# Layer-norm normalising on ScalarE, scale and shift on GpSimd, loads issued one by one, and a new timetable in a two-layer attention and expert kernel

## The chip, the cores and the metric

The kernel runs on one core of a Trainium2 chip. The metric is the device time of one execution in microseconds (us); lower is better. The core has TensorE (PE, its weight loads PEld), VectorE (DVE), ScalarE (ACT), GpSimd (POOL) and SyncE (SP), which here only issues DMAs.

## What is computed

Two pre-norm transformer layers run over x of shape (8, 512, 128), eight batches of 512 tokens of width 128. The reference, cut to its frame:

```python
def _layernorm(x, axis=-1, eps=1e-05):
    m = jnp.mean(x, axis=axis, keepdims=True)
    v = jnp.var(x, axis=axis, keepdims=True)
    return (x - m) / jnp.sqrt(v + eps)

x = x + _L0_attn_ref(_layernorm(x), wq, wk, wv, wo)          # causal, 16 heads of 8, 4 key heads
x = x + _L0_ffn_ref(_layernorm(x), router_w, router_b, w1, w2)     # 8 experts, top 1, silu(a) * g
x = x + _L1_attn_ref(_layernorm(x), W_q, W_dkv, W_uk, W_uv, W_o, ln_gamma, ln_beta)  # latent of 32, own norm, rotary
x = x + _L1_ffn_ref(_layernorm(x), gate_w, gate_b, w1, b1, w2, b2) # 8 experts, top 2, relu
```

The latent of layer 1's attention (512 x 32 a batch) is normalised too, and then multiplied by ln_gamma and shifted by ln_beta.

## The kernel before

The residual X stays in SBUF, 128 tokens of a tile on the partitions, 4 tiles a batch. Attention goes batch by batch, 16 in all (8 of layer 0, then 8 of layer 1). Each batch has a preparation (`prep`: statistics, normalise, transpose, projections, splitting q and k into three bf16 parts, parking these in DRAM and loading them back as stacks), a first pass over the scores for the row maxima (`max`, `m_hi`, `m_mid`, `m_park`, `m_load`), a second pass with Exp and the values (`score`, `values`, `normalise`), and the output projection (`turn_ctx`, `project`). After `project` comes the second norm of the layer (`stats`, `norm`, `turn` with x = "half") and the router's logits. The experts work on half the tokens at a time: group g = 0 is batches 0 to 3, g = 1 batches 4 to 7. When the fourth batch of a group is through, DVE chooses experts and places (`route`, `choose`, `places`), POOL scatters the rows in expert order to DRAM (`scatter`, 16 indirect DMAs in layer 0, 32 in layer 1), SP loads them back four tiles at a time (`fetch`), PE works slot by slot (`first`, `second`; 23 slots a group in layer 0 and 39 in layer 1, with a weight fetch `fetch_w1` each), and POOL gathers the results (`combine`, 16 or 32 indirect DMAs), each added to X by DVE. Layer 1's attention of a group needs layer 0's `combine` of that group. The kernel ends with layer 1's `combine` of g = 1 and its stores.

There are 40 layer norms: 16 of x = "xn" and 16 of "half" (four tiles of 128x128 each) and 8 of "lat" (four of 128x32). Each is: DVE bn_stats and bn_aggr on four tiles and var + eps (L1488 to L1493); POOL pow(-0.5) over 4 columns (L1025 to L1027); POOL four times (x - mean) * rs (L1049 to L1050), for "lat" also times gamma (L1054) and plus beta (L1056); PE transposes the result (L1125 or L1167). The small statistics have two buffers (`ln_small`), `xn` has one.

Every engine runs a list of steps of its own, in order, fixed when the kernel is built. `schedule()` gives each step a nominal time from constants (FIRST_SCORES, LENGTHS, AHEAD, HURRY, SCATTER, EXPERTS_AFTER, SLOT, COMBINE, W1_AHEAD). `Plan.make_orders` then simulates the engines with the costs in PARTS and the landing times in LANDS, and puts next the step that could start first; a tie goes to the lower nominal time. So nominal times are priorities, and costs decide which steps look ready. Only `set_ones`, `load_rest`, `fill` and `load_expert` (NOT_BEFORE) aren't put ahead of their nominal time. On the chip a step waits on semaphores, and what stands behind it on its engine waits too.

`load_rest` is a single step of SP at nominal 40.0: it issues 21 DMAs in a row, X of batches 2 to 7 and 15 weight and table loads (L886 to L893). The `fill` steps (L895 to L900) write zeros to the DRAM that the scatters go to, 10 DMAs of up to 512 KB, of which FILLS puts four at nominal 10 to 13.

## Time and profile before

| what | value |
|---|---|
| median of 3 runs | 1159.88 us (1159.86 to 1162.81) |
| the profiled execution's own time | 1159.01 us |
| its span in the trace | 1157.0 us |
| PE busy | 960.1 us, 83% |
| DVE busy | 696.5 us, 60% |
| POOL busy | 575.4 us, 50% |
| ACT busy | 562.1 us, 49% |

Busy time says how much an engine did, not what the end waited for. For that there are three views: the busy time of each engine in chosen stretches (where PE isn't full, something else holds the work up), the chain that ended last (followed back from the last instruction, at each step to what released it), and the instructions of one engine in order of time. Shares of the chain are given for a stretch. An SPq line is SP's time issuing DMAs.

### The profile page before, as it was taken

How to read it: one execution, taken by the hardware profiler on the slowest of the kernel's cores; microseconds unless marked ns; L12 is line 12 of the kernel's file. 1: busy time of each engine (PE TensorE's matmuls, PEld its weight loads, DVE VectorE, ACT ScalarE, POOL GpSimd, SP SyncE). 2: the span in 40 equal slices, each digit the busy share in tenths (PEclk: the TensorE clock that was granted, in tenths of full speed). 3: DMA queues.
4: the chain of work that ended last, by engine and by line, in shares of the span. 5: the costliest groups of instructions: out<-in, count | busy, mean ns of one | idle time of the engine just before them, and what ended most of it. 6: DMA issues, size and time to landing. Idle time of an engine off the chain costs nothing.

```text
span 1157.0 us, 26493 instructions
## 1 busy us (share of the span) xinstructions
PE 960.1 (83%) x9732; PEld 632.6 (55%) x9732; DVE 696.5 (60%) x1414; ACT 562.1 (49%) x987; POOL 575.4 (50%) x752
## 2 busy tenths in 40 slices
PE   3578889987999988887999988897989998887930
PEld 2334444544878545343887644443444687877930
DVE  2867776886556885778645787779768233123112
ACT  1056557663444443471454545454657854544610
POOL 4055544456211699456222399646884425455046
PEclk9999998987999988796999978897889999989975
DMA  4805432326654114316655204223441257778722
GB/s 135 191 26 160 111 94 68 90 63 185 205 161 124 49 50 112 84 58 176 197 159 160 52 20 121 85 59 79 139 121 53 69 145 205 217 219 239 199 67 73
DMA packets 148045, 139.42 MB, mean 121 GB/s; under 512 B 35056, under 2 KB 126544, under 8 KB 147920
## 3 DMA queue, kind: packets, MB, share of 16 engines
q1 hardware_dynamic: 141776, 125.13, 39.8%
q0 software_dynamic: 6144, 12.60, 3.8%
q8 instruction: 82, 1.34, 0.5%
q14 instruction: 43, 0.35, 0.1%
HBM read 94.82 MB, written 42.86 MB: 119 GB/s over the span
## 4 chain that ended last, share of the span: by engine, by line
PE 46%; POOL 21%; issue 10%; DVE 8%; DMA 6%; SPq 5%; ACT 5%; POOLq 0%; ACTq 0%; DVEq 0%
PE psum L1299 11%; PE psum L1232 9%; PE psum L1309 7%; POOL sorted_in L1095 7%; PE psum L1214 4%; POOL gathered L1105 4%; DVE neg_max L1452 4%; PE psum L1190 3%; ACT scratch L1398 3%; POOL scratch L1082 3%; POOL xn L1050 3%; DMA gathered<-sorted_out,rows_of 3%; PE psum L1161 2%; PE psum L1242 2%; POOL xn_half L1050 2%
## 5 line engine op out<-in xcount | busy, mean ns | idle before, releaser
L1452 DVE TENSOR_REDUCE neg_max<-psum 128x2 f32<-128x768 f32 (+3 forms) x352 | 382.6, 1120 | 103.5 <-PE psum L1195 101.1
L1398 ACT ACTIVATE scratch<-psum 128x1024 f32<-128x1024 f32 x320 | 317.5, 1027 | 122.7 <-PE psum L1214 121.3
L1082 POOL TENSOR_SCALAR_AFFINE_SELECT scratch<-scratch 128x512 f32<-128x512 f32 x256 | 159.4, 642 | 275.3 <-ACT scratch L1398 274.9
L1190 PE MATMUL psum<-k_stack,q_stack 48*128 48x128 bf16 (+3 forms) x1024 | 162.2, 339 | 47.9 <-DVE neg_max L1452 21.2
L1232 PE MATMUL psum<-scratch,values 128*32 128x512 f32 (+3 forms) x2048 | 183.3, 484 | 12.0 <-POOL scratch L1082 7.2
L1299 PE MATMUL psum<-rows_t,w_now 128*128 128x128 f32 x1360 | 176.1, 281 | 4.4 <-issue 1.9
L1299 PEld LDWEIGHTS psum<-rows_t,w_now 128*128 128x128 f32 x1360 | 163.4, 195 | 15.5 <-issue 13.0
L1309 PE MATMUL psum<-w,hidden_t 128*128 x992 | 139.7, 285 | 16.4 <-DVE rows_out L1449 12.3
L1214 PE MATMUL psum<-q_stack,k_stack 51*128 51x512 bf16 (+3 forms) x1024 | 126.2, 319 | 27.8 <-ACT scratch L1398 12.1
L1105 POOL DMA_INDIRECT gathered<-sorted_out,rows_of x96 | 92.8, 967 | 97.3 <-DMA sorted_out<-rows_out 66.1
L1309 PEld LDWEIGHTS psum<-w,hidden_t 128*128 128x128 f32 x992 | 123.5, 196 | 27.8 <-issue 27.2
L1434 ACT ACTIVATE hidden_t<-psum,w_now 128x128 f32<-128x128 f32 x312 | 88.4, 370 | 84.1 <-PE psum L1299 66.2
L1190 PEld LDWEIGHTS psum<-k_stack,q_stack 48*128 48x128 bf16 x1024 | 54.3, 101 | 117.9 <-issue 40.1
L1193 PE MATMUL psum<-masks_bf 64*128 64x128 bf16 x1024 | 118.3, 242 | 0.0
L1095 POOL DMA_INDIRECT sorted_in<-xn_half,rows_of x96 | 93.5, 974 | 46.8 <-issue 26.0
L1232 PEld LDWEIGHTS psum<-scratch,values 128*32 128x32 f32 x2048 | 59.2, 117 | 86.6 <-issue 53.0
L1195 PE MATMUL psum<-masks_bf 64*128 64x64 bf16 x1024 | 104.4, 206 | 0.0
L1449 DVE TENSOR_TENSOR rows_out<-psum,w_now 128x128 f32<-128x128 f32 x78 | 22.6, 292 | 115.0 <-PE psum L1309 114.9
L1317 ACT ACTIVATE ctx_raw<-psum 128x512 f32<-128x512 f32 x64 | 38.2, 597 | 103.2 <-PE psum L1232 103.1
L1214 PEld LDWEIGHTS psum<-q_stack,k_stack 51*128 51x128 bf16 x1024 | 36.7, 97 | 92.4 <-issue 39.9
L1195 PEld LDWEIGHTS psum<-masks_bf 64*128 64x128 bf16 x1024 | 58.5, 109 | 35.2 <-issue 14.0
L1679 DVE SCALAR_TENSOR_TENSOR X<-gathered,gate,X 128x128 f32<-128x128 f32 x96 | 38.2, 398 | 62.6 <-DMA gathered<-sorted_out,rows_of 60.9
(115 smaller groups left out, 1108.3 us busy)
## 6 DMA issues: line engine op xcount, KB each, us to landing
w_now<-in_w SPq DMA_DIRECT2D x78, 322.0 KB, 3.6
w_now<-in_w SPq DMA_DIRECT2D x46, 512.0 KB, 4.1
q_stack<-q_parts SPq DMA_DIRECT2D x64, 192.0 KB, 4.3
sorted_out<-rows_out SPq DMA_DIRECT2D x60, 128.0 KB, 3.5
rows_in<-sorted_in SPq DMA_DIRECT2D x28, 256.0 KB, 3.4
q_parts<-q_parts SPq DMA_DIRECT2D x16, 384.0 KB
k_stack<-k_parts SPq DMA_DIRECT2D x32, 192.0 KB, 3.7
sorted_in<-gathered SPq DMA_DIRECT2D x8, 512.0 KB, 5.1
```

Of the source, the lines that this page charges most:

```text
L1082: pool.affine_select(out=diag, in_=diag, compare_op=ALU.is_ge, fill=0.0, base=0, pattern=[[0, 4], [1, P]], channel_multiplier=-1).then_inc ...
L1095: pool.indirect_dma_start(sorted_in[g][:, :], bass.IndirectOffsetOnAxis(ap=rows_of[g][k][:, t:t + 1], axis=0), xn_half[:, t, :], None).the ...
L1105: pool.indirect_dma_start(gathered[s.slot][:, :], None, sorted_out[g][0:SLOTS[s.layer] * P, :], bass.IndirectOffsetOnAxis(ap=rows_of[g][k] ...
L1190: pe.matmul(out[:, j * width:end], q_stack[i][rows, pair, t * P:(t + 1) * P], k_stack[i][rows, k_of(layer, pair), 0:width], start=True, st ...
L1193: pe.matmul(out[:, end - P:end], ident_up[half, :], mask_up[half, :], start=False, stop=False)
L1195: ins = pe.matmul(out[:, end - P // 2:end], ident_low[half, :], mask_low[half, :], start=False, stop=True)
L1214: ins = pe.matmul(bank[u.bank + k][:, off:off + SEQ - j * P], k_stack[i][rows, k_of(layer, pair), j * P:(j + 1) * P], q_stack[i][rows, pai ...
L1232: ins = pe.matmul(bank[u.bank][CW * c:CW * c + CW, j * P:SEQ], values[batch_of(s) % 3][:, j, col:col + CW], p[:, c % 2, off:off + SEQ - j ...
L1299: ins = pe.matmul(bank[v.bank][:, c * P:(c + 1) * P], w1_now[layer][w.slot][:, n * FFN + c * P:n * FFN + (c + 1) * P], rows)
L1309: ins = pe.matmul(bank[u.bank][:, 0:P], hidden_t[h.slot][:, k * P:(k + 1) * P], w2[layer][:, bass.ds(e, 1), k * DIM:(k + 1) * DIM].rearran ...
L1398: act.activation(expd[s.slot], psum[:, u.bank:u.bank + 2, :], ACT.Exp, scale=SCALE).then_inc(read[u.bank], 1)
L1452: return dve.tensor_reduce(out=out, in_=in_, axis=AX, op=op, negate=negate)
```

## The change

- The normalising of all 40 norms goes from POOL to ACT: four `activation(Identity, scale=, bias=)` with the per-row scale rs and the per-row shift -mean * rs. POOL computes rs by pow as before and then the shift by a 128x4 multiply; DVE writes -mean in one more 128x4 instruction. For "lat" POOL still does gamma and beta behind ACT.
- One Tanh on one column at ACT's start, ahead of its wait for the constants.
- `load_rest` becomes 15 steps of one DMA at nominal 6.5 and on, 0.4 apart, and the X loads six steps `load_x` with times of their own (batches 2 and 3 at 5.5 and 6.0, 4 and 5 at 55 and 56, 6 and 7 at 90 and 91). All ten fills are now at 75 to 135.
- The constants of the timetable are set anew, and the planner's costs of `stats` and `norm` follow the new split.

```diff
-FILLS = (10.0, 11.0, 12.0, 13.0, 85.0, 95.0, 105.0, 115.0, 125.0, 135.0)
-FIRST_PREP, FIRST_SCORES = 8.0, 76.0
-AHEAD = (72.0, 82.0)
+REST_LOADS, REST_AT = 15, 6.5
+X_LOADS = (5.5, 6.0, 55.0, 56.0, 90.0, 91.0)
+FILLS = (75.0, 80.0, 85.0, 90.0, 95.0, 100.0, 105.0, 115.0, 125.0, 135.0)
+FIRST_PREP = 8.0
+FIRST_SCORES = 77.59
+AHEAD = (74.87, 87.27)
 LAG = 3.0
-LENGTHS = (36.0,) * 4 + (44.0,) * 8 + (38.0,) * 4
-GAP = 0.0
-HURRY = ((30.0, 30.0), (0.0, 30.0))
-SCATTER = ((1.8, 1.2), (1.4, 1.0))
-EXPERTS_AFTER = ((6.0, 6.0), (40.0, 6.0))
-SLOT = ((2.6,2.6),(4.2,2.4))
-COMBINE = ((1.6, 2.0), (2.0, 1.0))
+LENGTHS = (41.61, 37.6, 36.08, 35.9, 45.3, 45.3, 45.3, 41.6, 44.0, 44.0, 44.0, 44.0, 34.43, 38.0, 38.0, 38.0)
+GAP = 0.03
+HURRY = ((30.0, 30.0), (5.73, 36.79))
+SCATTER = ((1.8, 1.1), (1.73, 1.0))
+EXPERTS_AFTER = ((6.0, 5.52), (12.95, 6.0))
+SLOT = ((2.56, 2.6), (3.12, 1.47))
+COMBINE = ((2.44, 2.0), (2.0, 0.2))
...
-W1_AHEAD = 10.0
+W1_AHEAD = 8.06
...
-    table.put(40.0, "load_rest")
+    for b in range(2, BATCHES):
+        table.put(X_LOADS[b - 2], "load_x", x=b)
+    for n in range(REST_LOADS):
+        table.put(REST_AT + 0.4 * n, "load_rest", x=n)
...
-    "stats": (("dve", 1.6), ("pool", 1.1)), "norm": (("pool", 1.7),), "turn": (("pe", 0.55), ("act", 0.52)),
+    "stats": (("dve", 1.7), ("pool", 1.5)), "norm": (("act", 1.5),), "turn": (("pe", 0.55), ("act", 0.52)),
...
+        if s.kind == "norm" and s.x == "lat":
+            return (("act", 1.2), ("pool", 1.1))
...
                 if s.kind == "stats":
-                    small = ln_small[s.slot]
+
+                    scale, shift = (ln_small[s.slot][:, :, x:x + 1] for x in (8, 9))
                     pool.wait_ge(var_made, s.n + 1)
-                    pool.tensor_tensor(small[:, :, 9:10], small[:, :, 8:9], consts[:, C_HALF:C_HALF + QT].unsqueeze(2),
-                                       ALU.pow).then_inc(rs_made, 1)
+                    pool.tensor_tensor(scale, scale, consts[:, C_HALF:C_HALF + QT].unsqueeze(2), ALU.pow).then_inc(rs_made, 1)
+                    pool.wait_ge(rs_made, s.n + 1)
+                    pool.tensor_tensor(shift, shift, scale, ALU.mult).then_inc(stats_made, 1)
...
             act.wait_ge(values_set, 3)
+            act.activation(tanh_a[:, 0:1], values[0][:, 0, 0:1], ACT.Tanh)
             act.wait_ge(consts_loaded, 2 * DMA)
...
+                elif s.kind == "norm":
+                    of_it = of("stats", layer, b, s.x)
+                    small = ln_small[of_it.slot]
+                    act.wait_ge(stats_made, of_it.n + 1)
...
+                    for t in range(QT):
+                        ins = act.activation(out[:, t, :], src[:, t, :], ACT.Identity, bias=small[:, t, 9:10], scale=small[:, t, 8:9])
+                    ins.then_inc(normed, 1)
...
-                    dve.tensor_scalar(ve, mv[:, :, 1:2], EPS, None, ALU.add, ALU.bypass).then_inc(var_made, 1)
+                    dve.tensor_scalar(shift, mv[:, :, 0:1], -1.0, None, ALU.mult, ALU.bypass)
+                    dve.tensor_scalar(scale, mv[:, :, 1:2], EPS, None, ALU.add, ALU.bypass).then_inc(var_made, 1)
```

## Rows read from the trace of the kernel before

**Rows 1.** Windows by stage: stretch, busy us (instructions) per engine, PE clock, DMA.

```profile
0.00:68.00 68.00, 33.90 (x312) 19.11 (x312) 41.02 (x58) 7.26 (x17) 14.45 (x24) 1.00 0.60 149
68.00:285.00 217.00, 188.27 (x2268) 98.09 (x2268) 161.70 (x298) 129.82 (x185) 118.48 (x167) 0.90 0.38 100
285.00:385.00 100.00, 98.80 (x981) 81.56 (x983) 58.78 (x116) 45.91 (x65) 20.42 (x31) 1.00 0.52 149
385.00:545.00 160.00, 135.22 (x1344) 70.39 (x1338) 119.47 (x244) 77.30 (x109) 110.45 (x143) 0.82 0.35 92
...
650.00:887.00 237.00, 204.04 (x2221) 108.02 (x2221) 185.09 (x364) 130.88 (x180) 172.97 (x224) 0.86 0.32 84
...
945.00:1005.00 60.00, 53.34 (x438) 51.14 (x437) 17.55 (x64) 31.96 (x109) 31.18 (x33) 0.97 0.69 203
1005.00:1112.00 107.00, 88.83 (x687) 83.32 (x685) 21.98 (x74) 50.61 (x171) 30.57 (x32) 0.94 0.74 203
```

**Rows 2.** The page's part 4: chain that ended last, by engine and line.

```profile
PE 46%; POOL 21%; issue 10%; DVE 8%; DMA 6%; SPq 5%; ACT 5%; POOLq 0%; ACTq 0%; DVEq 0%
PE psum L1299 11%; PE psum L1232 9%; PE psum L1309 7%; POOL sorted_in L1095 7%; PE psum L1214 4%; POOL gathered L1105 4%; DVE neg_max L1452 4%; PE psum L1190 3%; ACT scratch L1398 3%; POOL scratch L1082 3%; POOL xn L1050 3%; DMA gathered<-sorted_out,rows_of 3%; PE psum L1161 2%; PE psum L1242 2%; POOL xn_half L1050 2%
```

**Rows 3.** Windows: two stretches with layer 0's gathers.

```profile
400.00:450.00 50.00, 39.86 (x330) 19.56 (x328) 35.74 (x104) 25.44 (x38) 47.48 (x60) 0.83 0.25 66
675.00:725.00 50.00, 43.76 (x420) 21.98 (x412) 38.65 (x98) 29.01 (x41) 45.44 (x59) 0.84 0.31 79
```

**Rows 4.** Windows of L1050 alone (the normalising on POOL).

```profile
400.00:450.00 50.00, 14.93 (x20) 0.83 0.25 66
...
675.00:725.00 50.00, 13.77 (x20) 0.84 0.31 79
```

**Rows 5.** SP's issues in time: start, us, instruction.

```profile
47.74 4.22 SPq L871 DMA_DIRECT2D X<-in_x  x6
...
60.48 0.43 SPq L950 DMA_DIRECT2D max_parts_out<-max_parts  x1
...
66.27 0.40 SPq L950 DMA_DIRECT2D max_parts_out<-max_parts  x1
```

**Rows 6.** POOL in time, the same stretch.

```profile
51.29 0.42 POOL L1072 TENSOR_TENSOR max_parts<-max_rest,max_parts 32x128 bf16<-32x128 f32 x1 [18.93 <-ACT max_parts L1317]
```

**Rows 7.** All engines in time, at the start.

```profile
9.20 3.14 POOL L1050 TENSOR_SCALAR xn<-X,ln_small 128x128 f32<-128x128 f32 x4
...
24.05 1.41 SPq L900 DMA_DIRECT2D sorted_in<-gathered  x2
```

**Rows 8.** Groups: line, busy us, mean ns, idle before.

```profile
L1434 ACT ACTIVATE hidden_t<-psum,w_now 128x128 f32<-128x128 f32 x312 | 88.4, 370 | 84.1 <-PE psum L1299 66.2 <-PE psum L1309 17.8
...
L1027 POOL TENSOR_TENSOR ln_small<-ln_small,consts 128x4 f32<-128x4 f32 x40 | 42.1, 1054 | 44.2 <-DVE ln_small L1493 43.5
L1317 ACT ACTIVATE ctx_raw<-psum 128x512 f32<-128x512 f32 x64 | 38.2, 597 | 103.2 <-PE psum L1232 103.1
...
L1493 DVE TENSOR_SCALAR ln_small<-ln_small 128x4 f32<-128x4 f32 x40 | 15.5, 388 | 1.4
...
L1054 POOL TENSOR_TENSOR lat_n<-lat_n,ln_gb 128x128 f32<-128x128 f32 x8 | 3.7, 456 | 0.7
...
L1317 ACT ACT_TABLE_LOAD x1 | 1.3, 1283 | 13.7 <-PE psum L1125 13.7
```

**Rows 9.** ACT in time: one slot's four activations.

```profile
967.85 1.15 ACT L1434 ACTIVATE hidden_t<-psum,w_now 128x128 f32<-128x128 f32 x4 [2.70 <-PE psum L1299]
```

**Rows 10.** Windows of L1299 alone (8 records a slot in layer 1).

```profile
887.00:939.00 52.00, 12.57 (x96) 11.43 (x96) 1.00 0.26 70
939.00:1005.00 66.00, 28.27 (x210) 25.93 (x211) 0.97 0.69 201
```

**Rows 11.** POOL in time: first scatter and first gather of layer 1's last stages.

```profile
962.13 1.10 POOL L1095 DMA_INDIRECT sorted_in<-xn_half,rows_of  x1 [16.79 <-DVE rows_of L1635]
...
1020.10 0.98 POOL L1105 DMA_INDIRECT gathered<-sorted_out,rows_of  x1 [17.68 <-DMA sorted_out<-rows_out]
```

More of the change, by code:

```diff
@@ L293 @@
 PARTS_MAX = ((("pe", 0.55), ("dve", 1.15)), (("pe", 0.38), ("dve", 1.15)), (("pe", 0.25), ("dve", 0.88)), (("pe", 0.3), ("dve", 1.15)))
-LANDS = {"load_rest": 8.0, "fill": 5.0, "load_expert": 5.0, "park": 2.8, "stacks": 4.6, "m_park": 1.8, "m_load": 2.0, "scatter": 2.4,
+LANDS = {"load_rest": 8.0, "load_x": 5.0, "fill": 5.0, "load_expert": 5.0, "park": 2.8, "stacks": 4.6, "m_park": 1.8, "m_load": 2.0, "scatter": 2.4,
          "fetch_w1": 4.6, "fetch": 3.0, "second": 2.4, "combine": 2.5}
@@ L386, in needs @@
                 return done("dve", of("combine", 0, b // GB, b % GB, (QT * (b % GB) + QT - 1, 0)))
-            return done("sp", of("load_rest")) if b > 1 else []
+            return done("sp", of("load_x", x=b)) if b > 1 else []
         if s.kind == "norm":
+            if engine == "pool":
+                return []
             out = done("pool", of("stats", layer, b, x))
@@ L398, in needs @@
         if s.kind == "turn" and engine == "pe":
-            return done("pool", of("norm", layer, b, x))
+            return done("act", of("norm", layer, b, x))
         if s.kind in ("q0", "kv0"):
@@ L408, in needs @@
         if s.kind in ("lat", "rotate") and x != "k" and engine == "pe":
-            return done("act", of("turn", 1, b, "xn"))
+            out = done("act", of("turn", 1, b, "xn"))
+            return out + (done("pe", of("lat_turn", 1, b - 1)) if s.kind == "lat" and b else [])
         if s.kind == "lat":
@@ L469, in needs @@
             if engine == "pe":
-                return done("act", of("turn", layer, b, "half")) + (done("sp", of("load_rest")) if n == 0 else [])
+                return done("act", of("turn", layer, b, "half")) + (done("sp", of("load_rest", x=REST_LOADS - 1)) if n == 0 else [])
             return self.route_before(s)
@@ L479, in needs @@
         if s.kind == "scatter":
-            return done("dve", of("places", layer, b)) + done("pool", of("norm", layer, GB * b + x, "half")) + done("sp", of("fill", x=len(FILLS) - 1)) + (
+            return done("dve", of("places", layer, b)) + done("act", of("norm", layer, GB * b + x, "half")) + done("sp", of("fill", x=len(FILLS) - 1)) + (
                 done("sp", of("fetch", 0, b, (SLOTS[0] - 1) // 4)) if layer else [])
@@ L567, in ready @@
                 old = self.users["small"][-2]
-                at = max(at, self.of("norm", old.layer, old.b, old.x).done.get("pool", LATE))
+                at = max(at, self.of("norm", old.layer, old.b, old.x).done.get("act", LATE))
             if engine == "pe" and s.kind in RING_OF and not (s.kind == "values" and s.y) and not (s.kind == "first" and s.layer and s.x % 2):
@@ L1049, in _ @@
-                    for t in range(QT):
-                        ins = pool.tensor_scalar(out[:, t, :], src[:, t, :], small[:, t, 6:7], small[:, t, 9:10], ALU.subtract, ALU.mult)
-                    if s.x == "lat":
-                        ins.then_inc(lat_steps, 1)
-                        pool.wait_ge(lat_steps, 2 * b + 1)
-                        pool.tensor_tensor(out, out, ln_gb[:, 0:1, :].to_broadcast([P, QT, LATENT]), ALU.mult).then_inc(lat_steps, 1)
-                        pool.wait_ge(lat_steps, 2 * b + 2)
-                        ins = pool.tensor_tensor(out, out, ln_gb[:, 1:2, :].to_broadcast([P, QT, LATENT]), ALU.add)
@@ L1163, in _ @@
                 elif s.kind == "lat_turn":
-                    pe.wait_ge(normed, of("norm", 1, b, "lat").n + 1)
+                    pe.wait_ge(lat_made, b + 1)
                     room(u)
@@ L1358, in _ @@
                     copy(parts_of[s.x][:, 1, 0:n], rest_of[layer, s.x][:, 0:n]).then_inc(mid_made, 1)
+                elif s.kind == "norm":
+                    of_it = of("stats", layer, b, s.x)
+                    small = ln_small[of_it.slot]
+                    act.wait_ge(stats_made, of_it.n + 1)
+                    src = X[:, QT * b:QT * b + QT, :]
+                    if s.x == "xn":
+                        out = xn[:, :, :]
+                        if (layer, b) != (0, 0):
+                            v = of("turn", layer if b else 0, b - 1 if b else BATCHES - 1, "xn").uses[0]
+                            act.wait_ge(full[v.bank], v.filled)
+                    elif s.x == "half":
+                        x, g = b % GB, b // GB
+                        out = xn_half[:, QT * x:QT * x + QT, :]
+                        if (layer, g) != (0, 0):
+                            act.wait_ge(scattered[x], rows_sent(layer if g else 0, g - 1 if g else 1, x))
+                    else:
+                        src = out = lat_n[:, :, :]
+                    for t in range(QT):
+                        ins = act.activation(out[:, t, :], src[:, t, :], ACT.Identity, bias=small[:, t, 9:10], scale=small[:, t, 8:9])
+                    ins.then_inc(normed, 1)
                 elif s.kind == "lat":
```

62 lines of the change are left out of this document (25 added, 37 removed).

## The prediction

> **What bounds the kernel now.** I read the windows by stage first [rows 1]. PE is full where experts run beside attention (98.80 of 100 us from 285 to 385), so nothing but less PE work shortens that stretch. In the stretches of attention without experts no engine is full: 68 to 285 has PE 188 of 217, DVE 162, ACT 130, POOL 118; 385 to 545 has PE 135 of 160 and POOL 110; 650 to 887 has PE 204 of 237 and POOL 173. There the order of handovers sets the pace. The clock column agrees: 0.90, 0.82 and 0.86 where PE pauses, 1.00 in the full stretch. The first 68 us (PE 33.90) are preparation of batch 0. From 945 on the last routing, the scatters, the second group of experts and the gathers follow one another, and the last norm is over by then.
>
> Then the chain that ended last [rows 2]: PE 46%, POOL 21%, "issue" 10%, DVE 8%, SPq 5%, ACT 5%. POOL's normalising (L1050) is 3% for xn and 2% for xn_half, some 5% of 1157 = 58 us (46 to 69 with rounding). So the moved work stands on the chain, though POOL is busy only half the time. Two stretches are worse than the mean: from 400 to 450 and 675 to 725, where layer 0's gathers meet layer 1's preparations, POOL is busy 47.48 and 45.44 of 50 us and PE only 39.86 and 43.76 [rows 3]; L1050 is 14.93 and 13.77 of it [rows 4]. Last the issues of SP at the start: the loads of `load_rest` begin at 47.74 and the next other issue, `m_park` of batch 0's first maxima, is at 60.48 [rows 5], while POOL had those maxima ready at 51.29 + 0.42 = 51.7 [rows 6]. They wait 8.8 us for nothing but SP's queue.
>
> **The sum is made against the profiled execution's own time, 1159.0 us** (span 1157.0, 2.0 around it); the median of the runs is 0.9 above it.
>
> **1. Loads at the start.** The 21 issues leave the place between the stacks and `m_park` and go to where SP waits for POOL's first parts (nominal 5.5 to 12.5), or to 55 and later. The first `m_park` comes 8.8 us sooner. Two early fills (1.41 us of SP at 24.05, just ahead of k's park [rows 7]) go too, and the table load of 1283 ns [rows 8] leaves the path of batch 0's transpose, since the new Tanh makes it while ACT has no work. Batch 0's norm is 3.14 us on POOL now [rows 7] and about 2 after. Everything up to the first stack so comes 1.4 + 1.3 + 1 = 3.7 us sooner, and the first scores 8.8 + 3.7 = 12.5. But the second `m_park`, at 66.27 [rows 5], hangs more on DVE's maxima than on SP: its share is the 3.7 plus little. Between 3.7 and 12.5 I take **-9**, nearer the upper end, since the first two quads of scores then run under the second half's maxima. What is late next is DVE, 41.02 us busy in the 68 [rows 1].
>
> **2. Fills moved.** Four more fills now stand among the stacks of 75 to 135. At 0.7 us each (half of the 1.41 for two [rows 7]) that is 2.8 us of SP, and each moves 512 KB that stack loads may meet: 0 to 6 us. SP waits most of that time: **+1**.
>
> **3. The norms.** POOL loses 3.14 us a norm and keeps pow at 1.05 us [rows 8]. It gains a multiply of 128x4. No row shows one: a 128x128 multiply takes 0.456, the pow of the same shape 1.05 [rows 8]. As pow is the slower operation and 128x128 more data, I take 0.45, and 1.05 as the upper end. ACT gains four 128x128 activations. No row has one with two per-row operands; four with one such operand take 1.15 us together [rows 9], and four copies of 128x512 would take 4 x 0.597 = 2.4 [rows 8]. The nearest is the first: 1.3. On the path a norm becomes 0.45 + 1.3 + 0.1 for a handover = 1.85 for 3.14, a saving of 1.3 (1.8 down to -0.4 at the ends).
>
> The skill would set this dearer. The Trainium skill, "ScalarE: Activation LUTs", section "What ACT_TABLE_LOAD costs", puts 186 ns + 0.833 a column, 93 for each pointer operand and an overlap of 93 between neighbours; for four with two pointers my estimate by that page is 1.64 us, and 1.27 for the case that the row has at 1.15. By the page item 3 would come out some 3 to 5 us worse; the row is already 10% under it.
>
> 58 us on the chain less batch 0's 3 are 55, or 55 / 3.14 = 17 norms: 17 x 1.3 = 22 us. When a chain shortens here, another takes over, as no engine is far below PE; I take half, -11. In the two POOL-full stretches (five norms each) POOL is relieved by 14.93 - 2.3 and 13.77 - 2.3, 24 us together, but PE's own work (39.86, 43.76) leaves at most 10.1 + 6.2 = 16 to gain; half of it, -8. Together **-19**, bounds -37 (22 of the chain, 16 there) and +5.
>
> Against it: ACT takes on about 32 x 1.3 + 8 x 0.9 = 49 us. ACT is on the chain for 5% = 58 us of its 562 busy, 10% of them; behind a waiting norm stand Exps of scores, for which PE's scores wait. That is **+5** (0 to +15). DVE does 40 more small instructions; L1493 takes 388 ns in the mean, so 15.5 us at most [rows 8], and of DVE's 696 us 8% of 1157 = 93 are on the chain: 15.5 x 0.13 = **+1** at most +2.
>
> **4. The timetable.** Mostly priorities among ready steps, so the PE-full stretches stay. One move has a size. Nominally layer 1's first experts start 697.2 before and 685.3 after, with batch 7's scores at 686.0 and 692.7, and a slot each 3.12 for 4.2. They are to go earlier against attention. Now 12 slots are done by 939, when attention ends, and 26 more by 1005 (96 / 8, 210 / 8 [rows 10]), at 66 / 26 = 2.5 us each; they cover exactly the time in which routing and scatters make the second group's rows. At the new rates some nine more would come first, nine times about 2 us of PE, less 5 us of idle PE there: the last batch up to 12 us later, PE then idle under the scatters. In return the gathers of the first group, which begin at 1020.10 [rows 11], can start sooner, and SLOT 1.47 puts the second group's slots ahead of them: PE is idle 107 - 88.83 = 18 us from 1005 to 1112 [rows 1] where they meet. +12 and up to -18: I take **0**.
>
> Sum: -9 + 1 - 19 + 5 + 1 + 0 = -21. 1159.0 - 21 = 1138, and 0.9 for the median: **1139 us**.
>
> **The rivals.** *The tail opens as well*: the gathers no longer stop the second group, and those 18 us go: 1139 - 18 = 1121. For it: PE has the idle time, and the first group's experts start sooner. Against: the gathers still stand behind 32 scatters on POOL (the first at 962.13 [rows 11]).
>
> *POOL's relief is taken up*: only the start and the two full stretches gain, and ACT's and DVE's costs stand: 1159.9 - 9 + 1 - 8 + 6 = 1150; with the stretches at nothing, 1158. For it: ACT is in order and its norms wait for POOL's two steps; against: L1050's 5% of the chain.
>
> *Slower*: layer 1's first experts go so far ahead of attention that they leave the scatters uncovered. Each slot moved costs 2 us of PE ahead of the last batch and 2.5 of cover behind it. Idle PE of 5 us and item 3 pay for the first ones: from (1159.9 - 1139 + 5) / 2 = 13 moved slots on the kernel is slower than before. With 20 of the 26 moved: 1139 + 40 - 5 = 1174. It takes the 3.12 spacing being kept while attention slips.
>
> *Not what it says*: if Identity lived in another table than Exp, each norm would bring two loads of 1.28 us, 40 x 2.57 = 103 us of ACT, about 1240. One load in the whole trace, with Copy, Exp, Tanh and Relu in turn [rows 8], speaks against it. The Trainium skill says in the same page, "Table sets: the hidden batching unit", that identity is in every set; no run here shows it yet.
>
> **How the numbers follow.** 1139 (1128 to 1149) has 0.42, the open tail 0.21, relief taken up 0.20, slower 0.13, the table 0.01, and 0.03 for none of these. The range reaches down over most of the open tail with item 3 at a better value, to 1105, and up over the whole of the third case, to 1163; the slower case and the table are left out. A measurement of this kernel tells about 0.3%, 3.5 us, from no change. Faster by more than that: 0.42 + 0.21 + 0.14 of the third case + 0.01 = 0.78. Same: 0.06 of the third case. Slower: 0.16.
>
> **What would show it.** Right for 1: no SP issues between stacks and the first `m_park`, the first Exp of scores 9 to 13 us sooner. For 3: four Identity activations near 1.3 us together, a POOL multiply under 0.5, POOL well under 45 of 50 in the two gather stretches with PE above 42 and 45. For 4: slots done by attention's end (12 now), and the idle PE after it. Wrong: more than one table load, ACT idle behind POOL's multiply ahead of Exps, PE idle for tens of us under the last scatters.

## The result and the profile after

The changed kernel takes **1110.0 us** (median; 1108.6 to 1116.8) beside 1159.9 of the kernel before on the same chip: a ratio of 0.958 [0.953, 0.962], so about 50 us less. The profiled execution took 1108.9 us. The forecast was 1139 with a range of 1105 to 1163: the sign is right, the range holds the time, and the gain is more than twice the 21 us of the sum.

The page of the kernel after: span, busy time by engine, granted clock in 40 slices, then the chain that ended last by engine and by line. It answers [rows 2].

```profile
span 1107.1 us, 26573 instructions
...
PE 934.3 (84%) x9732; PEld 623.3 (56%) x9732; DVE 691.2 (62%) x1454; ACT 617.4 (56%) x1148; POOL 466.9 (42%) x632
...
PEclk9759999996999998998999989997899998889975
...
PE 56%; DVE 13%; POOL 10%; issue 8%; DMA 6%; ACT 6%; SPq 1%; POOLq 0%; ACTq 0%; DVEq 0%
PE psum L1294 13%; PE psum L1227 11%; PE psum L1304 10%; DVE neg_max L1470 8%; PE psum L1209 5%; PE psum L1185 4%; ACT scratch L1416 4%; POOL sorted_in L1090 4%; DMA gathered<-sorted_out,rows_of 3%; POOL gathered L1100 3%; PE psum L1237 2%; POOL scratch L1077 2%; PE psum L1120 1%; PE psum L1262 1%; PE psum L1188 1%
```

POOL fell from 575 to 467 us of busy time and from 21% to 10% of the chain, PE rose to 56%. But PE's busy time fell too, from 960 to 934 us, with the same 9732 matmuls. No term of the sum allowed for that.

Windows of the kernel after (columns as in [rows 1]). Its stages end earlier than before's, so the stretches from 274 on are cut where nearly the same work stands (the last one at the same matmuls of attention, counted from the start).

```profile
0.00:68.00 68.00, 45.62 (x374) 26.27 (x376) 48.03 (x86) 17.59 (x42) 13.26 (x24) 0.82 0.53 136
...
274.00:370.00 96.00, 96.00 (x910) 79.49 (x908) 52.35 (x101) 47.46 (x69) 14.55 (x24) 1.00 0.54 156
370.00:509.00 139.00, 120.88 (x1372) 65.35 (x1370) 122.08 (x277) 91.48 (x150) 86.53 (x115) 0.92 0.40 106
...
618.00:839.00 221.00, 194.69 (x2244) 105.07 (x2242) 181.82 (x376) 150.40 (x241) 138.96 (x185) 0.92 0.34 88
```

The PE-full stretch is still full (100 us before with 981 matmuls, 96 now with 910). The stretches of attention without experts shrank: 160 us to 139 (1344 and 1372 matmuls), and 237 to 221 (2221 and 2244). In them the mean granted clock rose from 0.82 to 0.92 and from 0.86 to 0.92. The clock of the first stretch can't be compared: no clock is recorded before 73 us in before's trace and before 40 us in after's, and the views put 1.00 there (see B).

Where the 50 us came from can be read off the ends of batches (the start of `project`'s writing of `X`, us from the span's start, one trace each):

| | batch 1 | batch 3 | batch 7 | batch 11 | batch 15 | end |
|---|---|---|---|---|---|---|
| before | 152.1 | 232.1 | 499.2 | 771.5 | 938.8 | 1157.0 |
| after | 148.5 | 220.3 | 468.9 | 728.6 | 902.7 | 1107.1 |
| gained so far | 3.6 | 11.8 | 30.3 | 42.9 | 36.1 | 49.9 |

So 12 us come in the first four batches, 31 in batches 4 to 11, where attention meets experts and gathers, -7 in batches 12 to 15, where more expert slots are done now, and 14 after attention.

PE's waits before (for what it waited: us in total, times, longest).

```profile
PE psum L1190 <- DVE neg_max L1452: 21.2, 42, 2.0
PE psum L1125 <- POOL xn L1050: 16.9, 5, 12.5
PE psum L1190 <- ACT scratch L1398: 14.7, 29, 1.1
...
PE psum L1214 <- ACT scratch L1398: 12.1, 23, 1.1
...
PE psum L1190 <- DMA q_stack<-q_parts: 10.3, 1, 10.3
PE psum L1232 <- POOL scratch L1082: 7.2, 9, 1.5
```

The same after.

```profile
PE psum L1185 <- DVE neg_max L1470: 23.6, 51, 1.2
PE psum L1277 <- DMA rows_in<-sorted_in: 15.3, 1, 15.3
PE psum L1120 <- ACT xn L1375: 11.2, 1, 11.2
PE psum L1227 <- POOL scratch L1077: 9.9, 7, 3.0
PE psum L1185 <- ACT scratch L1416: 9.7, 21, 1.1
PE psum L1209 <- ACT scratch L1416: 9.5, 21, 1.4
```

PE waits for the Exps of scores (`ACT scratch`) 19.2 us instead of 26.8, though ACT has 55 us more to do. The waits for norms are gone but for batch 0's (16.9 - 12.5 = 4.4 us), and so is the wait for batch 0's stack (10.3). A new one, 15.3 us, is for the first rows of the second expert group. Half of the 50 us is busy time of PE (960.1 - 934.3 = 26), the other half its idle time.

PE isn't the only one that waited for norms. DVE's statistics of a norm need the buffer back that the norm two places before them reads. Before, and after:

```profile
DVE ln_small L1488 <- POOL xn L1050: 17.3, 6, 4.7
...
DVE ln_small L1506 <- ACT xn L1375: 1.9, 1, 1.9
```

DVE stood 17.3 us behind the norms of `xn` on POOL, and stands 1.9 us behind those on ACT.

### The profile page after: what moved, and what is told of

The parts are those of the page before. It is cut to its first block, busy times and chain, and to the rows that moved or that the text cites. A ratio compares the mean times of both kernels' runs of the same rounds, so it can differ in the third digit from the quotient of the medians.

```text
span 1107.1 us, 26573 instructions
## 1 busy us (share of the span) xinstructions
PE 934.3 (84%) x9732; PEld 623.3 (56%) x9732; DVE 691.2 (62%) x1454; ACT 617.4 (56%) x1148; POOL 466.9 (42%) x632
## 4 chain that ended last, share of the span: by engine, by line
PE 56%; DVE 13%; POOL 10%; issue 8%; DMA 6%; ACT 6%; SPq 1%; POOLq 0%; ACTq 0%; DVEq 0%
PE psum L1294 13%; PE psum L1227 11%; PE psum L1304 10%; DVE neg_max L1470 8%; PE psum L1209 5%; PE psum L1185 4%; ACT scratch L1416 4%; POOL sorted_in L1090 4%; DMA gathered<-sorted_out,rows_of 3%; POOL gathered L1100 3%; PE psum L1237 2%; POOL scratch L1077 2%; PE psum L1120 1%; PE psum L1262 1%; PE psum L1188 1%
## 5 line engine op out<-in xcount | busy, mean ns | idle before, releaser
L1185 PE MATMUL psum<-k_stack,q_stack 48*128 48x128 bf16 (+3 forms) x1024 | 156.3, 328 | 34.7 <-DVE neg_max L1470 23.6
L1227 PE MATMUL psum<-scratch,values 128*32 128x512 f32 (+3 forms) x2048 | 173.7, 464 | 12.1 <-POOL scratch L1077 9.9
L1294 PE MATMUL psum<-rows_t,w_now 128*128 128x128 f32 x1360 | 179.2, 283 | 1.6 <-issue 1.0
L1294 PEld LDWEIGHTS psum<-rows_t,w_now 128*128 128x128 f32 x1360 | 165.1, 196 | 12.0 <-issue 10.3
L1188 PE MATMUL psum<-masks_bf 64*128 64x128 bf16 x1024 | 114.5, 235 | 0.0
L1190 PE MATMUL psum<-masks_bf 64*128 64x64 bf16 x1024 | 101.4, 200 | 0.0
```

Source lines behind the costliest of these rows:

```text
L1185: pe.matmul(out[:, j * width:end], q_stack[i][rows, pair, t * P:(t + 1) * P], k_stack[i][rows, k_of(layer, pair), 0:width], start=True, st ...
L1188: pe.matmul(out[:, end - P:end], ident_up[half, :], mask_up[half, :], start=False, stop=False)
L1190: ins = pe.matmul(out[:, end - P // 2:end], ident_low[half, :], mask_low[half, :], start=False, stop=True)
L1227: ins = pe.matmul(bank[u.bank][CW * c:CW * c + CW, j * P:SEQ], values[batch_of(s) % 3][:, j, col:col + CW], p[:, c % 2, off:off + SEQ - j ...
L1294: ins = pe.matmul(bank[v.bank][:, c * P:(c + 1) * P], w1_now[layer][w.slot][:, n * FFN + c * P:n * FFN + (c + 1) * P], rows)
```

## Experiments

In all of these the outputs are computed in full; where work is added, it writes a spare tile that nobody reads. Times are medians; ratios are to the kernel before on the same chip.

**A. The three parts, alone and in pairs.** The change is split into norms (ACT instead of POOL, with their entries in the planner's costs), loads (with their entries too) and timetable. Of each edit a few lines:

```diff
 # e1_norm_only: before + ACT normalises, POOL makes scale and shift
-    "norm": (("pool", 1.7),)
+    "norm": (("act", 1.5),)
 # e2_loads_only: before + single issues, fills from 75 us on
+REST_LOADS, REST_AT = 15, 6.5
+X_LOADS = (5.5, 6.0, 55.0, 56.0, 90.0, 91.0)
 # e3_timetable_only: before + these, FIRST_SCORES, GAP, W1_AHEAD and the expert constants
-AHEAD = (72.0, 82.0)
+AHEAD = (74.87, 87.27)
-LENGTHS = (36.0,) * 4 + (44.0,) * 8 + (38.0,) * 4
+LENGTHS = (41.61, 37.6, 36.08, 35.9, 45.3, 45.3, 45.3, 41.6, 44.0, 44.0, 44.0, 44.0, 34.43, 38.0, 38.0, 38.0)
```

> The kernel before with the normalising on ScalarE (the planner's costs of stats and norm, the 128x4 multiply on GpSimd, the early Tanh), but with the old loads, fills and timetable. Theory A (the move of the norms is most of the 49.9 us; my item 3 was priced too low): 1120 to 1130 us. Theory B (the orders that the new loads and timetable give are most of it; item 3 was about right): 1140 to 1150. Theory C (the parts only work together, since each move changes every engine's order): 1155 or slower.

> The kernel before with only the loads: 15 single issues at 6.5, X loads with times of their own, all ten fills from 75 on. My item 1 and 2 together said 8 us: 1152 by theory A and B alike. Theory C: about 1160, because the trace of after has its first Exp of scores no earlier (71.0 against 68.6 us) and gains only from batch 1 on.

> The kernel before with only the constants of the timetable (FIRST_SCORES, AHEAD, LENGTHS, GAP, HURRY, SCATTER, EXPERTS_AFTER, SLOT, COMBINE, W1_AHEAD). Theory A: within 6 us of 1160, as my item 4 said. Theory B: 1140 or faster. Theory C: slower than 1160, as they were chosen for other costs.

> After without its loads: the norms on ScalarE and the new timetable, but the block of 21 issues at 40 and four fills at 10 to 13. Theory A and B: 1118, that is after plus the 8 us of the loads. Theory C: 1125 or slower, if the timetable needs X of batches 2 and 3 early.

> The norms on ScalarE and the new loads and fills, with the old timetable. If the parts added up (norms alone -14.0, loads alone +12.1): 1158 us. If the loads pay only beside norms on ScalarE, as they did with the new timetable (1122.5 without them, 1110.0 with them): 1134.

> After with the norms back on GpSimd: new loads and new timetable. Added up from the single runs (+12.1 and +14.1): 1186 us. The move of the norms is then worth 76 us under these orders. If the loads suit this timetable whatever the norms do: 1162 (1174.4 less 12), and the move is worth 52.

| kernel | us | ratio [95%] | PE busy, same matmuls |
|---|---|---|---|
| before | 1160 | 1 | 960.1 |
| norms (e1) | 1146.2 | 0.985 [0.978, 0.992] | 963.0 |
| loads (e2) | 1172.4 | 1.010 [1.006, 1.013] | 975.6 |
| timetable (e3) | 1174.4 | 1.012 [1.007, 1.017] | 969.7 |
| norms + timetable (e4) | 1122.5 | 0.968 [0.963, 0.974] | 939.5 |
| norms + loads (e5) | 1132.7 | 0.975 [0.969, 0.981] | 955.6 |
| loads + timetable (e6) | 1160.1 | 0.999 [0.997, 1.002] | 965.3 |
| all three (after) | 1110.0 | 0.958 [0.953, 0.962] | 934.3 |

The parts don't add. Norms are worth 1.5% alone, 3.4% beside the new loads, 4.4% beside the timetable and 4.2% beside both. Loads cost 1.0% alone and bring 1.1% on top of the other two; the timetable costs 1.2% alone and brings 1.8% on top. Each of these two is a loss only by itself: beside one other part the loads bring 1.0% (e1 to e5) or 1.3% (e3 to e6), and the timetable 1.7% (e1 to e4) or 1.0% (e2 to e6).

One reason is how the kernel is made: the order of every engine comes out of the planner's costs and dates, so any part rewrites it. Of PE's 1332 planned steps, 1143 stand in before's order with the loads alone, 1020 with the norms alone, 858 with the timetable alone and 847 with all three (the longest series of steps common to both orders, from each kernel's own planner). e4 has 1283 of the 1332 in after's order, so the 12.5 us that the loads bring there come with nearly the same order on PE.

The loads show it best. At batch 3 they are 7.5 us ahead of before alone (224.6 for 232.1), and the all-three kernel is 8.5 ahead of e4 there (220.3 for 228.8). But alone the kernel has lost it by batch 11 (785.6 for 771.5), while with the others it ends 12.5 us ahead.

**B. What time on POOL and on ACT costs.** Spare work is put into the kernel after without a word to the planner, so that every other instruction keeps its place (all 1332 steps of PE in the same order, and those of ACT and POOL too): four instructions on constants for each norm, on POOL where scale and shift are made, or on ACT behind the norm. e13 has two for each instead of four.

```diff
 # e7_pool_more (e13_pool_half: range(QT // 2)), in "stats" on POOL, behind the shift
+                    for t in range(QT):
+                        n = LATENT if s.x == "lat" else DIM
+                        if more[0]:
+                            pool.wait_ge(spare_made, more[0])
+                        pool.tensor_scalar(spare[:, 0:n], consts[:, 0:n], consts[:, C_ONE:C_ONE + 1], consts[:, C_HALF:C_HALF + 1], ALU.subtract, ALU.mult).then_inc(spare_made, 1)
+                        more[0] += 1
 # e8_act_more: the same loop in "norm" on ACT, with ACT.Identity, bias and scale from consts
```

> After, with all orders kept, and GpSimd doing four more 128x128 tensor_scalar (four of 128x32 for lat) behind each shift, on constants into a spare tile: about the GpSimd time that the move took away, 3.2 us a norm, read by nobody. Theory A (GpSimd's time is what the move freed): 1135 us or slower, over half of the 50 us come back. Theory B (it was where the norms' own chain ran and how the orders fell, GpSimd has time to spare at 42% busy): under 1122.

> After with half of GpSimd's spare work (two instructions a norm for four, some 60 us for 117), orders kept. If each microsecond of GpSimd costs about the same (0.5 by the run with four): 1110 + 31 = 1141. If it only hurts once GpSimd's slack is used up: under 1125.

> After, with all orders kept, and ScalarE doing four more Identity activations behind each norm into a spare tile, one after the other (some 2 us a norm, 75 us in all). My item 3 priced ScalarE's added time at 0.1 of it: 7 us, 1117. If ScalarE's time lies on the path as often as GpSimd's did: 1140 or slower.

Measured: e7 1172.4 us, 1.011 [1.005, 1.017]; e13 1131.2, 0.974 [0.970, 0.979]; e8 1166.8, 1.004 [1.001, 1.008]. Of e7: busy time, the chain by engine, the spare work, one wait of PE.

```profile
PE 967.5 (83%) x9732; PEld 637.1 (54%) x9732; DVE 696.6 (59%) x1454; ACT 619.5 (53%) x1148; POOL 584.1 (50%) x792
...
PE 51%; POOL 20%; DVE 10%; issue 8%; DMA 5%; ACT 5%; SPq 1%; POOLq 0%; ACTq 0%; DVEq 0%
...
L1050 POOL TENSOR_SCALAR spare<-consts 128x128 bf16<-128x128 f32 (+1 forms) x160 | 117.1, 732 | 11.9
...
PE psum L1235 <- POOL scratch L1085: 32.0, 16, 4.0
```

Of e13, the wait that grew.

```profile
PE psum L1235 <- POOL scratch L1085: 17.1, 15, 3.0
```

Of e8, its busy time and the two waits that grew.

```profile
PE 963.2 (82%) x9732; PEld 635.7 (54%) x9732; DVE 692.8 (59%) x1454; ACT 687.0 (59%) x1308; POOL 466.9 (40%) x632
...
PE psum L1187 <- ACT scratch L1424: 25.4, 36, 2.7
...
PE psum L1211 <- ACT scratch L1424: 21.9, 31, 3.2
```

117 us of POOL, at 42 to 50% busy, cost 62 us: 0.53 for each. The first 60 (e13) cost 0.0167 x 1160 = 19 us, the next 57 cost 0.0363 x 1160 = 42: the price rises with the load, from 0.3 to 0.7 us for each. 70 us more of ACT busy time cost 57, 0.8 for each. The traces say through what. In e7 the masks of scores (`affine_select`) stand behind the spare work, PE waits for them 32.0 us instead of 9.9 (17.1 in e13), and PE's busy time goes up from 934.3 to 967.5 (948.3): 22 + 33 = 55 of the 64 us that the span grew. In e8 the Exps stand behind it: 47.3 us of waiting for 19.2, and 963.2 of busy time: 28 + 29 = 57 of 60.5.

The busy time goes with the clock. The values matmuls of 128x512, one form with 512 records, before:

```profile
L1232 PE MATMUL psum<-scratch,values 128*32 128x512 f32 x512 | 78.8, 691 | 5.8 <-DVE max_rest L1449 3.4 <-POOL scratch L1082 1.0 <-DVE X L1449 0.5
```

and the same form after:

```profile
L1227 PE MATMUL psum<-scratch,values 128*32 128x512 f32 x512 | 73.9, 651 | 5.4 <-POOL scratch L1077 3.3 <-DVE ctx_n L1467 1.1 <-DVE max_rest L1467 0.5
```

They take 691 ns before, 651 after and 672 in e7. In these traces the granted clock stands at one of two levels, full (2.4 GHz) or half (1.2 GHz). The masks' matmuls of 128 columns tell which it is, in before from 60 to 68 us and from 84 to 110 (least, median and most ns):

```profile
L1193 PE MATMUL psum<-masks_bf x18: 307/311/312, 59.9 to 67.2; 64*128 64x128 bf16 x18
...
L1193 PE MATMUL psum<-masks_bf x54: 216/216/218, 83.9 to 105.6; 64*128 64x128 bf16 x54
```

They take 216 ns at the full clock and 311 at the half. So the first 73 us of before, where no clock is recorded and [rows 1] have 1.00, ran at half, at the least from the first such matmul on. Counted so in every trace (half up to the first record), PE is busy at the half clock for 204 us before, 145 after and 218 in e7. Half of this time is what the half clock can cost, and the busy time less that half is 858 us before, 862 after, 859 in e7, and 858 to 865 in all twenty traces. PE's busy time so differs by the time at the half clock and by little else. That the waits themselves bring the clock down is not shown: no run took it apart, and e16 below has a lower clock in a stretch where PE is idle for no longer.

e6 has its norms on POOL and e7 the spare work, with POOL almost equally busy (573.6 and 584.1), and e7 is 12 us slower. If orders made no difference, this would be what ACT's 56 us and DVE's extra instructions cost on that path, less what the shorter norm gains, and the norms' move, 50 us in company, would split into about -62 for the relief of POOL and +12 for the rest. But between e6 and e7 the planned order differs too (1080 of PE's 1332 steps in common), so the split is argued and not shown.

Nor do POOL's norms reach PE mainly by the way that e7's spare work takes. PE's wait for masks is 12.4 us in e6 and 9.9 after (7.2 before), so the masks hold 2.5 of the 50 us. From e6 to after PE's busy time falls by 31 us (965.3 to 934.3), its waits for Exps by 11 (30.1 to 19.2) and those for norms by 5 (16.7 to 11.9). By what links the norms on POOL delayed PE and the Exps is open.

**C. Is it the work, or what the planner thinks of the work?** Before, the planner priced a norm at 1.7 us on POOL, where [rows 7] show 3.14. e9 corrects only that price in the kernel before, e14 in e6; e10 and e11 tell the planner of the spare work of e7 and e8. The smaller norm of `lat` gets its own price in each: 2.9, 3.6 and 2.8 us.

```diff
 # e9_before_cost (kernel before), e14_norm_back_planned (e6)
-"norm": (("pool", 1.7),)
+"norm": (("pool", 3.2),)
 # e10_pool_more_planned (e7)
-"stats": (("dve", 1.7), ("pool", 1.5))
+"stats": (("dve", 1.7), ("pool", 5.0))
 # e11_act_more_planned (e8)
-"norm": (("act", 1.5),)
+"norm": (("act", 3.5),)
```

> The kernel before, with one thing changed: the planner's cost of a norm on GpSimd is 3.2 us (lat 2.9), as the trace shows it, for 1.7. The instructions are the same, in other orders. Theory D (the orders were laid for a norm of half its length, and the move repaired the plan as a side effect): 1145 us or faster, much of what the norms' move gives by itself (1146). Theory E (GpSimd's time itself is what costs): 1155 to 1165.

> New loads and timetable with the norms on GpSimd (1160.1 with the planner's 1.7 us a norm), and the planner told of the true 3.2 us. Theory D (part of the move's gain is a plan that no longer mistakes a norm's length): 1140 to 1150. Theory E (engine time alone): 1155 to 1165.

> After with GpSimd's spare work as before (1172), but the planner told of it (stats on GpSimd 5.0 us, lat 3.6). Theory D: most of the 62 us come back, 1130 or faster. Theory E: the time stays lost, 1155 or slower.

> After with ScalarE's spare work as before (1167), but the planner told of it (norm on ScalarE 3.5 us, lat 2.8). Theory D: 1130 or faster. Theory E: 1150 or slower.

Measured: e9 0.982 [0.978, 0.986], e14 1158.5 us, 0.995 [0.991, 0.998], e10 1175.3, 1.011 [1.004, 1.018], e11 1187.9, 1.027 [1.020, 1.033]. The single times of e9 spread more widely than those of any other kernel (1132 to 1162). Its 0.982 goes by the four fastest of ten; by the medians of all, 1151.2 and 1160.9, it is 0.992. So e9 gains between 0.8% and 1.8%.

Telling the planner doesn't pay for the work: e10 is level with e7, and e11 is even 2% slower than e8. So a wrong date isn't what e7 and e8 lost their time by. But a right price for the norm brings the kernel before 0.8 to 1.8% with nothing moved, near what the whole move of the norms does alone (1.5%, by its interval 0.8 to 2.2). In company it is worth 0.5% (e6 to e14) at the edge of the noise, and 0.2% by the medians. So of the 4.2% of the norms' move the wrong price explains little; most of it needs the work itself to go.

**D. Which constants of the timetable.** Each starts from the kernel after.

```diff
 # e12_old_experts (layer 1's values as before)
+HURRY = ((30.0, 30.0), (0.0, 30.0))
+SCATTER = ((1.8, 1.1), (1.4, 1.0))
+EXPERTS_AFTER = ((6.0, 5.52), (40.0, 6.0))
+SLOT = ((2.56, 2.6), (4.2, 2.4))
+COMBINE = ((2.44, 2.0), (2.0, 1.0))
 # e18_experts_between
+EXPERTS_AFTER = ((6.0, 5.52), (26.0, 6.0))
+SLOT = ((2.56, 2.6), (3.6, 1.47))
 # e15_old_lengths: LENGTHS as before
 # e16_old_ahead: FIRST_SCORES = 76.0, AHEAD = (72.0, 82.0), GAP = 0.0
 # e17_ahead_layer1: AHEAD = (74.87, 82.0)
```

> After with layer 1's old constants only (HURRY, SCATTER, EXPERTS_AFTER 40, SLOT 4.2 and 2.4, COMBINE 1.0). The stages of the runs so far say: from the last project to the end 204 us with the new ones and 216 to 218 with the old; on the other side the last four batches of layer 1 take 3 to 17 us longer with the new ones. So 1118 to 1122 if the trade is the one that I put at nothing in item 4; 1110 or less if the earlier experts cost as much as they bring.

> After with layer 1's first experts between the two settings: EXPERTS_AFTER 26 for 12.95 (40 in the old), SLOT 3.6 for 3.12 (4.2 in the old). After leaves PE waiting 15.3 us for the last group's rows; the old setting leaves none, but four slots of the first group come after the last scatter and the gathers meet the second group. Between them both should be small: 1100 to 1106 us, faster than both. If the cover doesn't matter: 1110.

> After with the old LENGTHS only. Layer 1's constants gave nothing (1110.2), so the timetable's 20 us are in LENGTHS, in AHEAD and FIRST_SCORES, or in the rest. If LENGTHS: 1125 to 1132.

> After with the old AHEAD, FIRST_SCORES and GAP only, that is preparations with a nominal time 3 and 5 us nearer to their batch. If they hold the timetable's gain: 1125 to 1132; if LENGTHS does: 1112.

> After with AHEAD of layer 1 alone at its old 82.0 (87.27 in after). With both AHEADs, FIRST_SCORES and GAP old the kernel took 1133, and its trace was level with after's up to layer 0's last project (468.9 us in both) and lost 23 us in layer 1. If the lead of layer 1's preparations holds that: 1125 to 1133. If small changes of any constant lose 20 us by falling into other orders: it can't be told apart from that by this run alone, but a time near 1110 would point to the other three constants.

| kernel | us | ratio [95%] |
|---|---|---|
| after | 1110.0 | 0.958 [0.953, 0.962] |
| old experts (e12) | 1110.2 | 0.958 [0.953, 0.963] |
| experts between (e18) | 1104.8 | 0.952 [0.947, 0.956] |
| old lengths (e15) | 1133.1 | 0.975 [0.972, 0.977] |
| old ahead (e16) | 1133.1 | 0.974 [0.971, 0.977] |
| old ahead, layer 1 alone (e17) | 1125.7 | 0.968 [0.964, 0.973] |

The expert constants of layer 1 are worth nothing. With the old LENGTHS (e15), or with the old AHEAD, FIRST_SCORES and GAP (e16), the kernel loses 1.7%. These two don't add either: with all constants old (e5) it is 1.8% behind after, no more than with one of them. In e16 the trace is level with after to the last `project` of layer 0 (468.9 in both) and loses 23 us in layer 1's attention. Of after, from there to the last `project`:

```profile
469.00:903.00 434.00, 395.95 (x4211) 254.22 (x4204) 297.33 (x617) 267.48 (x455) 199.26 (x270) 0.94 0.41 115
```

Of e16, the same stretch, and the wait that grew:

```profile
469.00:926.00 457.00, 421.09 (x4266) 261.40 (x4265) 303.43 (x620) 274.14 (x461) 202.50 (x274) 0.89 0.39 109
...
PE psum L1209 <- DVE neg_max L1470: 17.5, 22, 3.0
```

All 23 us are PE busy time (421.09 for 395.95, with 55 matmuls more), at a granted clock of 0.89 for 0.94; PE is idle for 35.9 us of it, and for 38.0 of after's. The scores' wait for maxima is 17.5 us for 8.9 in the whole kernel. AHEAD dates a batch's preparation only, while its maxima keep their nominal distance to the scores, so this wait changed through the orders. With layer 1's AHEAD alone old (e17) 1.1% are lost.

Whether these constants are worth something by what they mean, or whether another order by any other cause would lose as much against after's, is not shown. e15 has 928, e16 1103 and e17 1161 of PE's 1332 steps in after's order; the two kernels that lose nothing have 1214 (e12) and 1279 (e18).

The experts' trade can be seen around the end of attention. Windows of after: the last batches, the scatters of the second group with the rest of the first group's slots, and the tail; then L1294 alone (8 records a slot) in the first two.

```profile
839.00:903.00 64.00, 63.11 (x616) 47.47 (x615) 18.13 (x48) 48.38 (x109) 13.35 (x22) 1.00 0.43 119
903.00:968.00 65.00, 46.29 (x366) 43.73 (x365) 18.60 (x71) 27.23 (x91) 31.96 (x34) 0.90 0.64 183
968.00:1060.00 92.00, 82.37 (x663) 78.36 (x663) 20.95 (x71) 49.47 (x166) 30.35 (x32) 0.94 0.76 210
...
839.00:903.00 64.00, 18.65 (x136) 16.44 (x136) 1.00 0.43 119
903.00:968.00 65.00, 21.88 (x160) 19.96 (x160) 0.90 0.64 183
```

e12, from the same start, cut at its own last `project` and last scatter:

```profile
839.00:890.00 51.00, 48.96 (x455) 35.32 (x447) 12.65 (x37) 38.14 (x79) 11.44 (x19) 0.93 0.25 67
890.00:955.00 65.00, 56.13 (x447) 53.06 (x446) 19.39 (x74) 34.12 (x114) 31.95 (x34) 0.95 0.71 205
```

e18, likewise:

```profile
839.00:896.00 57.00, 53.92 (x499) 38.00 (x499) 14.69 (x40) 39.94 (x85) 12.47 (x21) 0.94 0.28 77
896.00:957.00 61.00, 53.17 (x431) 50.22 (x430) 18.88 (x73) 32.77 (x110) 31.95 (x34) 0.94 0.70 204
```

By the count of [rows 10], after begins 19 slots before attention ends (136 records here and 16 just ahead of 839) where before and e12 begin 12 and e18 13. PE then idles 18.7 of 65 us under routing and scatters, 15.3 of them in the one wait for the first rows of the second group. e12 ends attention 13.4 us sooner (889.3 for 902.7), but 3.3 of these are there at batch 11 already (725.3 for 728.6), before any moved slot, so the moved slots hold 10. It idles 8.9, and from attention's end on it takes 10 us longer (214.6 for 204.4), with fewer slots done when the gathers begin. e18 lies between and idles 7.8; with 1104.8 us it is the fastest kernel of the study, 4.8% under before. Its lead over after is 0.6% with overlapping intervals, from runs on different occasions, so it isn't clear of the noise; the spans of the two traces are 1099.7 and 1107.1 us.

## Why the prediction was right in sign and wrong in size

That 1110 lies in the range is luck in the main: the range reached down to 1105 for an open tail, and most of the missing 29 us came from elsewhere.

**Item 1, loads (-9, and +1 for the fills): the size near at batch 3, the mechanism wrong.** A gain of 8 is there at batch 3: 7.5 us in e2, 8.5 from e4 to after. But the prediction's sign for it, the first Exp 9 to 13 us sooner, did not come. In time, the kernel after on DVE, SP and ACT:

```profile
38.96 18.59 DVE L1470 TENSOR_REDUCE neg_max<-psum 128x2 f32<-128x768 f32 x18 [0.44 <-PE psum L1190]
...
61.50 0.33 SPq L963 DMA_DIRECT2D max_parts_out<-max_parts  x1
...
71.04 4.81 ACT L1416 ACTIVATE scratch<-psum 128x1024 f32<-128x1024 f32 x5 [2.72 <-PE psum L1209]
```

The block of loads ahead of the first `m_park` is gone, as foreseen (two loads of X, 0.98 us from 60.08 on, stand there), yet it comes at 61.50 for 60.48 in [rows 5], right behind its data, which POOL has ready at 61.29. DVE now does 18 maxima in one go before it makes the first parts (23 before them in all, 12 before), and PE uses the time for batch 1 and 2 (45.62 us busy of the first 68 for 33.90 in [rows 1]). The first Exp is at 71.0, 2.4 us later than before's 68.6; with the norms alone (e1) it is at 66.2. So the wait behind SP's loads is gone, but the new order makes the maxima's parts later, and the gain appears only in the next batches. In e2 some 20 us are lost again from batch 3 to the end; by what is open.

**Item 3, the norms: this is the step that failed, together with adding up the items as if each had one price in every order.** The terms one by one. The price of a norm was nearly right. After, the groups that do it now (columns as in [rows 8]):

```profile
L1375 ACT ACTIVATE xn<-X,ln_small 128x128 f32<-128x128 f32 x64 | 26.3, 485 | 10.5 <-POOL ln_small L1043 10.5
...
L1375 ACT ACTIVATE lat_n<-lat_n,ln_small 128x32 f32<-128x32 f32 x32 | 10.6, 403 | 3.4 <-POOL ln_small L1043 3.4
L1511 DVE TENSOR_SCALAR ln_small<-ln_small 128x4 f32<-128x4 f32 x40 | 10.6, 264 | 1.4
...
L1043 POOL TENSOR_TENSOR ln_small<-ln_small 128x4 f32<-128x4 f32 x40 | 9.0, 224 | 3.1
...
L1316 ACT ACT_TABLE_LOAD x1 | 1.3, 1283 | 0.8 <-PEq L1751 0.8
```

Four activations take 1.65 us together (ACT from 9.41 on, batch 0), where I took 1.3, and the multiply takes 0.22, where I took 0.45: 1.87 + 0.1 for the hand-over is 1.97 for the 1.85 of the sum. DVE's one extra operation a norm is lost in the noise (691.2 us for 696.5 in all). One table load, as before. The estimate from the Trainium skill's "ScalarE: Activation LUTs", section "What ACT_TABLE_LOAD costs", was 1.64 us for this case and the trace agrees with its 1.65; the row of [rows 9], with one pointer operand, was the wrong neighbour for two. The same page's section "Table sets: the hidden batching unit" has identity in every set, and the single load agrees.

What failed is the step from the price to the path. I took L1050's own share of the chain, 58 us, let 1.3 of each 3.14 us go, and halved it to -11, with -8 for two stretches. With +5 for ACT and +1 for DVE that is -13. Measured, the move is worth -14 in before's timetable (e1) and -50 under the new loads and dates (e6 to after). So the price was near for the old timetable and 37 us short for the new loads and dates, which the change brings with it.

The share of the chain counts only the norms that themselves stood last, in one order. What is queued behind a norm on POOL, and DVE's statistics that waited for it (17.3 us), stand in the chain under other names. In after's orders B measured 0.53 us for each us of POOL's time: 62 us for 117, as much time as the norms took on POOL (51.1 + 50.5 + 15.4), against my 19. The halving for "another takes over" has no one number behind it: in after's orders the first 60 us cost 19 and the next 57 cost 42, while with before's timetable the whole move brought 14.

The second failed step is that PE's busy time was held fixed. In the two POOL-full stretches the sum let the kernel gain no more than PE's idle time (10.1 + 6.2), and nowhere had it a term for PE's own. That fell by 26 us, half of the result, with 59 us less of it at the half clock (204 to 145).

The sign "POOL well under 45 of 50" in the gather stretches did not come. The windows of [rows 3] reach beyond the gathers; cut at the first and last gather of a group, before and after are:

```profile
392.00:428.00 36.00, 29.10 (x291) 14.56 (x291) 31.23 (x74) 17.40 (x24) 31.18 (x40) 0.81 0.18 50
657.00:704.00 47.00, 40.96 (x388) 21.35 (x388) 36.88 (x82) 21.58 (x30) 40.52 (x50) 0.75 0.15 41
...
376.00:412.00 36.00, 31.32 (x338) 15.81 (x337) 32.89 (x75) 25.75 (x44) 30.74 (x40) 0.95 0.25 70
625.00:656.00 31.00, 25.23 (x298) 13.56 (x296) 28.33 (x79) 20.03 (x35) 26.65 (x34) 0.94 0.13 33
```

POOL is as busy while it gathers as it was (87 and 86% before, 85 and 86% after). The first group's gathers take 36 us as before, with 47 matmuls more beside them; the second group's take 31 us for 47.

**ACT (+5) and DVE (+1)**: probably too low for ACT. By the split over e7, which is argued, it is +12, and a further 70 us cost 57 (e8). DVE's term is 15.5 x 0.13 = 2.0 where the sum has 1, which changes little.

**Item 4, the timetable (0): right for the part that was worked out, and blind to the other.** For layer 1's experts I had "nine more slots first, up to 12 us later, up to 18 back, 0". There are 19 slots begun by attention's end for 12, so 7 more; attention ends 10 us later by them, the time behind it gives 10 back, and e12 is level with after. But "mostly priorities among ready steps" put LENGTHS and AHEAD at nothing without a reason, and after loses 20 us with the old values of either. The timetable as a whole costs 1.2% alone, and brings 1.0% beside the new loads, 1.7% beside the moved norms and 1.8% beside both.

**The rivals.** *POOL's relief is taken up* (1150) was the wrong way: in company POOL was worth more than its chain share. *The open tail* (1121) came in part: PE idles 9.6 of 92 us from 968 on, for 18 of 107 in [rows 1], but 12 us of new idling stand under the scatters (18.7 for 6.7 of 60). *Slower* was to decide from 13 moved slots on; 7 were moved. The table loads did not come.

The terms of the forecast beside what was measured: -9 + 1 for the loads (on top of the other two -12.5, alone +12), -13 for the norms with ACT and DVE (on top -50, alone -14), 0 for the timetable (on top -20, alone +14). Alone the three add up to +12, together they are -50, so 62 us belong to no part by itself. The forecast met the norms' value *alone*, and nowhere allowed for company.

## What to carry to other kernels

Where engines run in order on a schedule made ahead, don't take the price of an engine's work from its share of the chain alone: for each long instruction on a half-full helper engine ask which hand-over of the bounding engine is queued behind it. The spread is wide. Here each us added cost 0.3 to 0.8 us, more when the engine was busier, and taking 117 us off POOL brought 14 or 50 us, by the orders around it. When work leaves an engine, try new dates and costs of the schedule with it: the new dates alone were a loss of 1.2%, beside the moved norms a gain of 1.7%. A wrong price in the schedule (1.7 for 3.14 us here) is itself worth a look, for correcting it brought 0.8 to 1.8% with nothing else changed. A part tested alone tells little of its worth in company where each edit rewrites the whole order.
